# Three PSUM evictions of a two-layer adaLN kernel move from ScalarE to VectorE, with the places set anew

## The reference, cut to what matters

```python
# layer 0
h = _layernorm(x) * (1 + ca) + sa
x = x + ga * attention(h)        # one head: scores of h Wq and h Wk (D = 32), causal; zeros -> float32 min; softmax; times h Wvdown Wvup
h = _layernorm(x) * (1 + cb) + sb
x = x + gb * experts(h)          # probs = softmax(h Wg + bg); the best of 8 experts: relu(h We[e] + be[e]) * its prob
# layer 1
h = _layernorm(x) * (1 + ca) + sa
x = x + ga * attention(h)        # 16 heads of 8, no mask: softmax(q k^T) v, then Wout, bout
h = _layernorm(x) * (1 + cb) + sb
x = x + gb * ffn(h)              # two linear maps per batch: (h W1^T + b1) W2^T + b2
```

## Time and profile before

| | |
|---|---|
| median of 3 runs | 1714.13 us (1711.33 to 1717.23) |
| profiled execution | 1714.09 us, of which the span of the trace is 1712.8 |
| prologue, up to 129.7 us | PE busy 106.1, DVE 68.8, ACT 59.3 |
| one batch, 718.3 to 913.5 us | PE busy 189.3, DVE 178.2, ACT 169.0, POOL 92.7 of 195.2 |
| steps 58 to 64 of it, 848.6 to 860.5 | PE 11.6, DVE 10.2, ACT 10.5 of 11.9 |
| steps 65 to 71 of it, 860.5 to 871.3 | PE 9.9, DVE 8.5, ACT 10.1 of 10.8 |

### The profile page before, as it was taken

The page is one execution under the profiler, slowest core; times in us unless marked ns, Lnnn a source line. Parts: engine busy times, 40 slices in busy tenths (PEclk is TensorE's granted clock), DMA queues, the critical chain, the costliest instruction groups (busy, mean ns, idle before and its releaser), DMA issues.

```text
span 1712.8 us, 56705 instructions
## 1 busy us (share of the span) xinstructions
PE 1621.6 (95%) x24168; PEld 707.5 (41%) x24168; DVE 1482.1 (87%) x2256; ACT 1368.1 (80%) x1934; POOL 667.8 (39%) x1085
## 2 busy tenths in 40 slices
PE   6998999999999999999999999999999999999998
PEld 3754443344434443334434443334434443323335
DVE  5649988999889998899889998899989998989963
ACT  4443778988899878988899878988899887777784
POOL 2321345445444355444554365344554362102010
PEclk9999999999999999999999999999999999999999
DMA  2111211112120311012110311112110221111101
GB/s 74 52 56 36 63 32 55 33 53 65 56 64 19 97 57 55 28 45 76 58 58 19 89 49 55 46 47 77 42 58 23 74 58 42 52 33 46 37 27 32
DMA packets 83288, 87.22 MB, mean 51 GB/s; under 512 B 9452, under 2 KB 67484, under 8 KB 83036
## 3 DMA queue, kind: packets, MB, share of 16 engines
q1 hardware_dynamic: 82492, 83.07, 16.4%
q10 hardware_dynamic: 544, 0.52, 0.1%
HBM read 61.02 MB, written 21.99 MB: 48 GB/s over the span
## 4 chain that ended last, share of the span: by engine, by line
PE 63%; ACT 16%; DVE 14%; issue 4%; POOL 2%; DMA 1%; SPq 0%; ACTq 0%; POOLq 0%; DVEq 0%
PE pv_psum L809 21%; PE side_psum L537 15%; PE buffer L794 11%; ACT p L1040 10%; DVE row_max L1364 8%; PE buffer L784 7%; PE side_psum L627 2%; PE buffer L537 2%; PE side_psum L594 1%; PE pv_psum L819 1%; ACT o_sb L1049 1%; DVE st_f L1103 1%; ACT p0T L967 1%; POOL sm_f L1394 1%; POOL xn_f L1400 1%
## 5 line engine op out<-in xcount | busy, mean ns | idle before, releaser
L1364 DVE TENSOR_REDUCE row_max<-buffer 128x2 f32<-128x1024 f32 x1024 | 1219.6, 1217 | 118.7 <-PE buffer L784 107.0
L1040 ACT ACTIVATE p<-buffer 128x1024 f32<-128x1024 f32 x1024 | 1043.6, 1026 | 184.2 <-PE buffer L794 171.5
L809 PE MATMUL pv_psum<-p,v 128*9 128x256 f32 x8192 | 575.7, 382 | 4.1 <-ACT o_sb L1049 2.2
L784 PE MATMUL buffer<-k_ops,q_ops 24*128 24x512 f16 x2048 | 397.6, 385 | 29.5 <-ACT p L1040 22.0
L794 PE MATMUL buffer<-q_ops,k_ops 26*128 26x512 f16 x2048 | 397.1, 385 | 4.4 <-DVE row_max L1364 3.1
L809 PEld LDWEIGHTS pv_psum<-p,v 128*9 128x9 f32 x8192 | 155.2, 89 | 234.9 <-issue 150.2
L794 PEld LDWEIGHTS buffer<-q_ops,k_ops 26*128 26x128 f16 x2048 | 96.0, 91 | 350.9 <-issue 244.4
L784 PEld LDWEIGHTS buffer<-k_ops,q_ops 24*128 24x128 f16 x2048 | 96.0, 91 | 147.7 <-ACT p L1040 112.3
L1510 POOL TENSOR_SCALAR nm_parts<-nm 128x16 f16<-128x16 f32 x64 | 17.0, 266 | 351.3 <-DVE nm L1287 351.3
L1495 POOL TENSOR_TENSOR hm<-masks,hT_f 128x1024 f32<-128x1024 bf16 x56 | 120.1, 2150 | 64.0 <-PE side_psum L537 50.8
L537 PE MATMUL side_psum<-we,hm 128*32 128x128 f32 x3648 | 121.0, 274 | 0.0
(11 more groups left out here) (310 smaller groups left out, 1674.5 us busy)
## 6 DMA issues: line engine op xcount, KB each, us to landing
masks<-masks_rows SPq DMA_DIRECT2D x16, 1024.0 KB, 5.7
q_ops<-products SPq DMA_DIRECT2D x256, 48.0 KB
k_ops<-products SPq DMA_DIRECT2D x256, 48.0 KB
attention<-o_sb SPq DMA_DIRECT2D x248, 18.0 KB
x<-in_L_attn_inputs SPq DMA_DIRECT2D x8, 512.0 KB, 4.3
products<-q_parts SPq DMA_DIRECT2D x16, 256.0 KB, 2.2
w_sb<-in_L_ffn_W SPq DMA_DIRECT2D x16, 256.0 KB, 3.2
out<-x SPq DMA_DIRECT2D x16, 256.0 KB, 2.8
```

The source lines that it names most:

```text
L784: m = e.matmul(buffer[:, hh, :], q_ops[rows, slot, of, i * P:(i + 1) * P], k_ops[rows, slot, of, halves(half)[1]], start=True, stop=True)
L809: m = e.matmul(pv_psum[q:q + VW, half * QUARTER:(half + 1) * QUARTER], v1[b % 2][:, kb, 2 * hp + hh, :], p_sb[n % KEPT][:, hh, part * QUAR ...
L1040: e.activation(p_sb[n % KEPT][:, :, :], unit("exp", n)[0][:, :, :], ACT.Exp, scale=over_scale[n // (2 * PERIOD)]).then_inc(S["exp_done"], 1)
L1364: e.tensor_reduce(mx[pair % 2][:, :, i, half], unit("max", n)[0][:, :, :], axis=AX.X, op=ALU.max).then_inc(S["max_done"], 1)
```

## The change

`EMPTIED_BY` names DVE instead of ACT for three stages, gates, g0 and v1. Their stage functions move from the ScalarE program to the VectorE program with the same waits, `copy` becoming `tensor_copy`; these are 8 + 16 + 16 copies of 128x512 float32. Who waited for the gates in `side_act` now waits in `side_dve`. POOL's four memsets (`zero_rows`, for which the first SyncE loads of layer 0's expert weights wait) move to the start of its program. `SWITCH`, `LIGHT`, `PLACES`, `COUNTED`, `ZEROS_AHEAD` (288 fillers, now 341), `ZEROS_BESIDE` (141 before step 0, now 157; 134 behind, now 171) and `ALONE` have new numbers.

```diff
-EMPTIED_BY = {"gates": "act", "channels": "act", "g0": "act", ... "qk1": "act", "v1": "act",
+EMPTIED_BY = {"gates": "dve", "channels": "act", "g0": "dve", ... "qk1": "act", "v1": "dve",
-SWITCH, LIGHT = 1.2, 6.6
+SWITCH, LIGHT = 1, 6.2
...
-    "channels_b 7 0": 37, "channels 0 1 1": 52, "moe 0 4": 1, "moe_a 0 4": 10, "onehotT 0 1": 16, "scores 0 6 1": 4, "g0 1 1": 4, "times_v 1 0": 21,
+    "channels_b 7 0": 34, "channels 0 1 1": 49, "moe 0 4": 1, "moe_a 0 4": 29, "onehotT 0 1": 28, "scores 0 6 1": 4, "g0 1 1": 4,
...
@@ scalar_program
-        def g0_stage(b, half):
-            v = filled("g0", b, half)
-            if b:
-                act.wait_ge(S["side_filled"], side["scores", b - 1, T - 1, 1].filled)
-            e.copy(g0[:, halves(half)[1]], v).then_inc(S["side_act"], 1)
...
-        def v1_stage(b, half):
-            v = filled("v1", b, half)
-            act.wait_ge(S["pv_done"], (b - 1) * 2 * PERIOD)
-            e.copy(v1[b % 2][:, halves(half)[0], :, 0:DH], v.rearrange("p (t h d) -> p t h d", t=4, d=DH)).then_inc(S["side_act"], 1)
...
@@ vector_program
+        def gates_stage(b):
+            v = filled("gates", b)
+            if b >= 3:
+                dve.wait_ge(S["side_dve"], side["wff", b - 3].emptied)
+                for half in range(HALVES):
+                    dve.wait_ge(S[f"x2_{half}"], b - 2)
+            e.tensor_copy(gates[b % 3][:, :, :].rearrange("p j c -> p (j c)"), v).then_inc(S["side_dve"], 1)
+
+        def g0_stage(b, half):
+            v = filled("g0", b, half)
+            if b:
+                dve.wait_ge(S["side_filled"], side["scores", b - 1, T - 1, 1].filled)
+            e.tensor_copy(g0[:, halves(half)[1]], v).then_inc(S["side_dve"], 1)
+
+        def v1_stage(b, half):
+            v = filled("v1", b, half)
+            dve.wait_ge(S["pv_done"], (b - 1) * 2 * PERIOD)
+            e.tensor_copy(v1[b % 2][:, halves(half)[0], :, 0:DH], v.rearrange("p (t h d) -> p t h d", t=4, d=DH)).then_inc(S["side_dve"], 1)
...
         def wff_stage(b):
             v = filled("wff", b)
-            dve.wait_ge(S["side_act"], side["gates", b].emptied)
+            dve.wait_ge(S["side_dve"], side["gates", b].emptied)
...
@@ gpsimd_program (so also in wout_stage)
+        for v in (be3[:, :], onehotT[:, :], b2_sb[:, :], gate_sb[:, :, :]):
+            e.memset(v, 0.0).then_inc(S["zero_rows"], 1)
+
...
         def gates_stage(b):
-            pool.wait_ge(S["side_act"], side["gates", b].emptied)
+            pool.wait_ge(S["side_dve"], side["gates", b].emptied)
...
-        for v in (be3[:, :], onehotT[:, :], b2_sb[:, :], gate_sb[:, :, :]):
-            e.memset(v, 0.0).then_inc(S["zero_rows"], 1)
```

More of the change, by code:

```diff
@@ L181 @@
[L181 to L184 removed]
+apply 0 0 1, channels 0 0 0, g0 0 0, channels 0 0 1, gates 0, g0 0 1, scores 0 0 0, scores 0 1 0, exp0 0 0, v0 0, transpose_p 0 0 0, softmax 0 0,
@@ L901, in scalar_program @@
         early = {WEIGHTS_AT[0]: weights_natural, WEIGHTS_AT[1]: weights_late}
-        def gates_stage(b):
-            v = filled("gates", b)
-            if b >= 3:
-                act.wait_ge(S["side_dve"], side["wff", b - 3].emptied)
-                for half in range(HALVES):
-                    act.wait_ge(S[f"x2_{half}"], b - 2)
-            e.copy(gates[b % 3][:, :, :].rearrange("p j c -> p (j c)"), v).then_inc(S["side_act"], 1)
         def channels(b, which, half):
```

80 lines of the change are left out of this document (40 added, 40 removed), and 35 rows, old and new, of tables (COUNTED, ZEROS_AHEAD, ZEROS_BESIDE).

## The result

The changed kernel is **slower**: 1728.34 us median (1726.49 to 1729.62, 4 runs) beside 1714.08 before on the same chip, a ratio of 1.0088 [1.0067, 1.0110]. A second measurement beside other kernels gave 1.0096 [1.0078, 1.0115]. That is 14 to 16 us more, where 2 less were forecast and the range ended at 1722. The profiled execution took 1727.11 us, its span is 1725.8.

The account below looks back on a forecast made before the run. PE, DVE and ACT were taken to bound the kernel as a ring, none full, by stretches where one is late. From 1714.1 us, -2.4 steady and +0.6 prologue gave 1712.3, forecast 1712; range 1702 to 1722.

Parts of the forecast that it names:

- the ring and the stretches: PE, DVE and ACT pass lateness around through three PSUM buffers; stretches where a side stage delays one decide, not total busy time.
- The copies leave ACT: Steady steps: 32 copies each stop delaying an exponential by 0.13 us, at most 4.2 us; half taken, -2.1 us.
- The second copy of g: Steady batches: the first score product no longer waits 0.38 us for this copy's bank; half of 2.3 taken, -1.2 us.
- The copies arrive on DVE: Steps 58 to 64: added DVE work exceeds the stretch by 0.35 us a batch; 0.15 taken, +0.9 us in six batches.
- (e): Prologue scale computation: maxima, mask product and index searches move behind it on DVE, so the one-hot comes later, +2.2 us.
- (b): Prologue, batch 1's first score product: eleven fillers ahead go, -1.3 us; 29 more stand ahead of the later transposition, +1.3; together 0.
- (d): Prologue, last expert: the v1 product and copy of v move behind it, so its ending activation gains, -0.8 us.
- (a): Prologue, first score copy: it no longer queues on ACT behind a copy of g, -0.4 us.
- (c): Prologue, ahead of the second half's channels: 49 fillers for 52, -0.4 us where PE is late.
- (f): POOL's memsets go to its start and SyncE's loads start earlier; no row shows anyone waiting for them, 0.
- The last batch's fillers: Last batch's steps: 171 fillers for 134 stand beside waiting time; 0 taken, ends -1 and +2 us.
- Rival 2: Slower, about 1724 us: DVE becomes the limit of steps 58 to 64, +2.06 us a batch; chance 0.19.

Follow-up runs that it names:

- gates_only: The kernel before with only the eight copies of the gates on VectorE, its tables unchanged; 1713.6 us, ratio 1.0006.
- before_steps: The kernel before with the changed kernel's PLACES, COUNTED, SWITCH and LIGHT, copies still on ScalarE; 1725.2 us, ratio 1.0083.
- after_pro: The changed kernel with the prologue order and the fillers ahead of stages and before step 0 as before, early memsets kept; 1726.0 us, ratio 1.0077.
- after_counts: The changed kernel with COUNTED, SWITCH and LIGHT of before, so value products are spread otherwise over the same places; 1736.5 us, ratio 1.0143.
- after_zb: The changed kernel with the fillers beside the steps from step 832 on as before (134, not 171); 1726.3 us, ratio 1.0085.

## Why the prediction was wrong, point by point

Three steps of the prediction failed. It priced a moved copy by its own engine's time and put the rest at nothing. It had no term for the value products that the same tables spread anew. And it put the reset fillers at 0, in the last batch and, together, in the prologue. The first failed in kind but weighs little in the changed kernel (+0.11 us a batch at step 40, not 0; it is 1.0 in before's places). The second cost some 0.5 us and more a steady batch, the third 3.4 us in steps 832 to 959 and a part of the 3.5 of the prologue.

1. **What bounds the kernel**: the ring and the stretches held as far as the runs show. The steady batches, 195.19 us, moved by 0.5 in the one followed. One row was read wrong: the last window of the earlier trace rows, 11.50 us, holds steps 72 to 79. Steps 72 to 78 take 9.94 us, with DVE busy 9.26, the same 93%.
2. **"The copies leave ACT", -2.1 us**: the 0.13 us by which a copy delays the exponential was read rightly, and gates_only bears it out in size (0.1 gained in steps 63 to 65, and given back). It is the wrong question. A side bank's copy has two followers, the next exponential on its own engine and the next side product on PE, and PE's queue has the exp product behind that. I priced the first.
3. **"The second copy of g", -1.2**: not isolated by a run. The products' wait of 2.3 us is gone, and a weight load of the transposition waits 2.6 in six. Steps 65 to 71 are 0.4 shorter and 72 to 78 0.2 longer, with value products moved in both, so at most about 0.2 us a batch came.
4. **"The copies arrive on DVE", +0.9**: the duration, 0.67, was 0.68 to 0.69. For steps 58 to 64 I added up 12.25 us of DVE work and took 0.15 of the 0.35 over. The stretch takes 12.25, but with DVE busy 11.85, so that the equal number is partly chance; the two stretches together, 58 to 71, take 0.06 more. And "at step 40 a copy comes and a pair of statistics goes: nothing" failed in the term that was not in it, the ffn product's wait for the bank: +0.11 even with the statistics gone, +0.46 with them.
5. **Steady sum, -0.4 a batch; measured +0.4 to +0.9**, 1.7 in batch 1. Of that surplus 0.9 lies in steps 16 to 23, where PE stands 0.78 us ahead of a product of `numer` (408.03) and POOL, which makes it, had waited 4.1 us for a DMA (4.2 before). Kernels with before's prologue, before_steps and after_pro, do not have this surplus; its cause is open. The largest part of the steady loss, +0.5 in steps 80 to 87, was in no term at all: I followed the moved copies and not the value products, which the same tables had moved. after_counts bears that out for the whole batch.
6. **The prologue, +0.6; measured +3.5**, though before's profile had a low stretch there (95 to 99 us) and the changed kernel's none. (e) is right for the one-hot, +2.2, and wrong in the sum: undone, it gives the first maximum 0.8, and the ratios show no gain. (b) failed: the 11 fillers' 1.33 us stood in front of a stop of 1.7 us and gave nothing, and the 29 others stood on the chain with all their 3.33 us, for the 1.3 that I had counted; the transposition behind them comes at 98.62 for 94.82. (d) gave 1.1 for 0.8: the activation that ends the experts comes 1.7 late, at 108.01, where the one-hot was 2.8 late. Behind it, fillers added 1.1 where I had looked at no row. (a), (c) and (f) no run isolates.
7. **The last batch's fillers, 0 with an end of +2**: the mis-sized term with the largest share. Steps 768 to 1023 lost 6.6 us; 3.4 of them by the fillers with their clock stretch, 1.3 in steps 784 to 831, and some 2 in the last batch. The 1.3 are not the places' alone, for before_steps and after_pro have them too and lose 0.2 and 0.3 there. The 2 are not the fillers': before_steps and after_zb, with before's fillers, lose 1.7 and 2.1 there.
8. **Rival 2** had the right sign and nearly the right total, 1724, by a mechanism that is not there. Steps 58 to 64 take 12.25 us and not 14, and DVE's idle time in them fell from 1.71 to 0.40. Its evidence was the right one for v1, though, the wait of 0.83 us behind a bank that DVE empties: what it showed was PE's loss, not DVE's. The rule of the Trainium skill ("Perfetto Trace Analysis", Identifying the Most-Contended Engine), to relieve the engine of highest occupancy, gave the right sign for this change, though DVE's occupancy, 87% before and after, did not set the time: in before's places g's and the gates' 24 copies on DVE cost 0.2 us a batch, v1's 16 cost 0.9, and with before's spread in the new places all forty cost nothing that the steady batches show.

## What to carry to other kernels

When an eviction changes engine, price what stands ahead of it in the new engine's queue and what PE has queued behind the bank that it frees; a wait there is paid by every product behind it, while the engine's own share of 0.1 us is small. Where tables are reset along with it, compare all that they move, step by step: here the value products and fillers outweighed the forty copies. Time of fillers, or of anything on the chain, is not gained by taking it out before you know what would stand there instead. And look at the mean clock of every execution, not only at the profiled one.
